# Second attention stage with rows of 3125 columns instead of 3200, and a last block of 53 rows

## The reference

```python
h = (x @ W).reshape(N, H, HD)
al_src = jnp.einsum('nhd,hd->nh', h, a_src)
al_dst = jnp.einsum('nhd,hd->nh', h, a_dst)
e = jax.nn.leaky_relu(al_src[src] + al_dst[dst], 0.2)
emax = jax.ops.segment_max(e, dst, num_segments=N)
ex = jnp.exp(e - emax[dst])
denom = jax.ops.segment_sum(ex, dst, num_segments=N)
out = jax.ops.segment_sum((ex / denom[dst])[:, :, None] * h[src], dst, num_segments=N)
...
y = _layernorm(out.reshape(N, DIM) + gat_b + res)
return _layernorm(jax.nn.gelu(y @ W1 + b1) @ W2 + b2 + y)
```

## Time and profile before

| | |
|---|---|
| median of 3 runs | 4212.96 us (4205.56 to 4214.2) |
| profiled execution | 4210.95 us, its span 4209.2 us |
| PE busy over the span | 3842.8 us, 91% |
| DVE | 2343.3 us, 56% |
| ACT | 2062.7 us, 49% |
| POOL | 589.5 us, 14% |
| L1027 and L1037 on DVE, 100 each | 355.1 us and 354.9 us |

### The profile page before, as it was taken

The page is one execution under the profiler, slowest core; times in us unless marked ns, Lnnn a source line. Parts: engine busy times, 40 slices in busy tenths (PEclk is TensorE's granted clock), DMA queues, the critical chain, the costliest instruction groups (busy, mean ns, idle before and its releaser), DMA issues. The chain is left out here.

```text
span 4209.2 us, 75724 instructions
## 1 busy us (share of the span) xinstructions
PE 3842.8 (91%) x27713; PEld 2926.6 (70%) x27714; DVE 2343.3 (56%) x4742; ACT 2062.7 (49%) x3697; POOL 589.5 (14%) x595
## 2 busy tenths in 40 slices
PE   4999969999999999599998888889979998996999
PEld 2555536666666666377777776678868887885888
DVE  7999835555555555399998898600002220002665
ACT  1555536666666666388887788500000010002554
POOL 0000001111111111100005566400000000000222
PEclk9999979999999999799999999999989998997999
DMA  2555562222222322433242332165644435554342
GB/s 66 213 228 220 212 205 96 103 84 106 103 84 96 108 88 71 167 111 107 98 169 89 102 104 88 62 182 145 146 146 150 147 128 179 145 145 152 141 145 99
DMA packets 185141, 550.29 MB, mean 131 GB/s; under 512 B 44903, under 2 KB 148529, under 8 KB 151217
## 3 DMA queue, kind: packets, MB, share of 16 engines
q1 hardware_dynamic: 184096, 540.23, 37.5%
q10 hardware_dynamic: 784, 6.55, 0.5%
HBM read 374.52 MB, written 172.19 MB: 130 GB/s over the span
## 5 line engine op out<-in xcount | busy, mean ns | idle before, releaser
L2005 PE MATMUL g_acc<-g_r,g_ct 128*128 128x256 f32 (+1 forms) x3750 | 862.9, 383 | 61.3 <-DMA g_r<-d_r 19.9
L931 ACT ACTIVATE a_sm<-a_p_t 128x1024 f32<-128x1024 f32 (+1 forms) x800 | 668.5, 836 | 370.6 <-PE a_p_t L874 370.4
L888 PE MATMUL a_p_o<-a_sm,a_v 128*64 128x128 f32 x10000 | 749.1, 281 | 85.6 <-ACT a_sumT L938 85.6
L888 PEld LDWEIGHTS a_p_o<-a_sm,a_v 128*64 128x64 f32 x10000 | 555.5, 137 | 377.1 <-issue 212.7
L2005 PEld LDWEIGHTS g_acc<-g_r,g_ct 128*128 128x128 f32 x3750 | 704.5, 192 | 161.2 <-issue 68.8
L874 PE MATMUL a_p_t<-ident,a_sm 128*128 128x128 f32 x5000 | 715.5, 281 | 41.3 <-ACT a_sm L925 26.1
L925 ACT ACTIVATE a_sm<-a_sm,a_negm 128x1024 f32<-128x1024 f32 (+1 forms) x600 | 706.8, 1178 | 85.0 <-DVE a_negm L991 84.6
L1011 DVE CUSTOM_DVE_ANT_0 a_sm<-a_p_s,a_full 128x400 f32<-128x400 f32 x800 | 429.3, 572 | 485.9 <-PE a_p_s L860 481.6
L874 PEld LDWEIGHTS a_p_t<-ident,a_sm 128*128 128x128 f32 x5000 | 559.1, 142 | 151.1 <-issue 128.0
L860 PE MATMUL a_p_s<-a_kt,a_q 64*128 64x400 f32 x1600 | 401.5, 560 | 34.2 <-DMA a_full<-d_logs 21.9
L1027 DVE SCALAR_TENSOR_TENSOR a_sm<-a_a_bc,a_al 128x3200 f32<-128x3200 f32 x100 | 355.1, 3551 | 34.0 <-DMA a_a_bc<-d_as 15.8
(11 more groups left out here) (244 smaller groups left out, 3926.7 us busy)
## 6 DMA issues: line engine op xcount, KB each, us to landing
a_mask<-d_full SPq DMA_DIRECT2D x75, 1600.0 KB, 6.8
g_ct<-d_ct SPq DMA_DIRECT2D x75, 1600.0 KB, 8.2
d_logs<-logs SPq DMA_DIRECT2D x25, 1664.0 KB, 6.9
a_full<-d_logs SPq DMA_DIRECT2D x25, 1664.0 KB, 7.5
d_ct<-ct SPq DMA_DIRECT2D x25, 1600.0 KB, 5.3
d_full<-a_full SPq DMA_DIRECT2D x25, 1600.0 KB, 5.4
a_a_bc<-d_as SPq DMA_DIRECT2D x10, 1600.0 KB, 9.6
a_q<-d_q SPq DMA_DIRECT2D x100, 64.0 KB, 2.2
```

The source lines that it names most:

```text
L888: m = nc.tensor.matmul(p_o[r:r + HD, 0:P], v[:, a, (p * heads + h) * HD:(p * heads + h + 1) * HD], sm[buf][:, a * P:(a + 1) * P], start=a ...
L931: nc.scalar.activation(sm[buf][:, a_row[u] * P:a_row[u + 1] * P], p_t[u % 2][:, 0:turns[u] * P], ACT.Copy).then_inc(s_copy, 1)
L2005: t = nc.tensor.matmul(acc[par][:, 0:width], ct[par][:, a * P:(a + 1) * P], r[:, a, :], start=a == 0, stop=a == NT - 1)
```

## The change

In the second attention stage (`dot` false) the row that is computed ends at column 3125 instead of 3200. Both DVE instructions get 3125 columns, the last part of the exponential 1077 instead of 1152. The last block of a row has 53 columns: it is turned as 128 rows by 53 columns into 53 rows of `p_t`, 53 rows are copied back, and 53 rows of `v` and of the turned block are multiplied. Loads, table sizes, buffers, semaphores and the first stage are as they were (in the first stage `width` is NPAD, so that every expression has its old value). The lines of the changed file are 3 or 4 higher.

```diff
+        width = NPAD if dot else N
+        exps = EXPS[:-1] + [width]
...
+        rows_in = lambda a: min(P, width - a * P)
...
-                        m = nc.tensor.transpose(p_t[u % 2][:, i * P:(i + 1) * P], sm[buf][:, a * P:(a + 1) * P], ident[:, :])
+                        m = nc.tensor.transpose(p_t[u % 2][0:rows_in(a), i * P:(i + 1) * P], sm[buf][:, a * P:a * P + rows_in(a)], ident[:, :])
...
-                        m = nc.tensor.matmul(p_o[r:r + HD, 0:P], v[:, a, (p * heads + h) * HD:(p * heads + h + 1) * HD], sm[buf][:, a * P:(a + 1) * P],
+                        m = nc.tensor.matmul(p_o[r:r + HD, 0:P], v[0:rows_in(a), a, (p * heads + h) * HD:(p * heads + h + 1) * HD], sm[buf][0:rows_in(a), a * P:(a + 1) * P],
...
-                    c = slice(EXPS[e], EXPS[e + 1])
+                    c = slice(exps[e], exps[e + 1])
...
-                    nc.scalar.activation(sm[buf][:, a_row[u] * P:a_row[u + 1] * P], p_t[u % 2][:, 0:turns[u] * P], ACT.Copy).then_inc(s_copy, 1)
+                    n_rows = rows_in(a_row[u + 1] - 1)
+                    nc.scalar.activation(sm[buf][0:n_rows, a_row[u] * P:a_row[u + 1] * P], p_t[u % 2][0:n_rows, 0:turns[u] * P], ACT.Copy).then_inc(s_copy, 1)
...
-                    v_.scalar_tensor_tensor(sm[buf][:, :], a_bc[:, h, 0, :], al[gp][:, g:g + 1], a_bc[:, h, 1, :], ALU.add, ALU.max).then_inc(s_lift, 1)
+                    v_.scalar_tensor_tensor(sm[buf][:, 0:N], a_bc[:, h, 0, 0:N], al[gp][:, g:g + 1], a_bc[:, h, 1, 0:N], ALU.add, ALU.max).then_inc(s_lift, 1)
...
-                    v_.tensor_tensor_reduce(out=sm[buf][:, :], in0=sm[buf][:, :], in1=mask[gp][:, :], scale=1.0, scalar=-3.0e38,
+                    v_.tensor_tensor_reduce(out=sm[buf][:, 0:N], in0=sm[buf][:, 0:N], in1=mask[gp][:, 0:N], scale=1.0, scalar=-3.0e38,
                                             op0=ALU.add, op1=ALU.max, accum_out=mx[:, buf % 2, 0:1]).then_inc(s_sfree, 1)
```

## The result

The changed kernel takes 4228.44 us (median of 8 runs, 4214.84 to 4232.3) where the kernel before takes 4208.48 (8 runs, 4203.68 to 4214.2). The ratio is 1.0043, 95% interval 1.0033 to 1.0052: slower, and outside the range that was given. The profiled execution has a span of 4228.3 us against 4209.2.

What follows compares the result with a forecast made beforehand. DVE was taken to bound the first stretch, DVE and the loop of PE and ACT in turn the second. Gains of 8.0 and 2 us from 4211 gave 4201, plus 2 for the median: 4203 us, range 4195 to 4219.

Steps and rivals of the forecast that it cites:

- DVE's 0.16 us a unit: DVE's two instructions, 3200 to 3125 columns: 0.16 us a unit less, 8.0 us over the first stretch's 50 units.
- The exponential: ACT's last exponential, 1152 to 1077 columns: 0.06 us a unit less, hidden in the first stretch, once a tile in the second.
- The copy and the last weighing of 53 rows: ACT's last copy and PE's last weighing, 53 rows for 128: nothing gained; for the weighing 0.17 us as upper bound.
- The last turn: PE's last turn, loading 53 columns of weights: 0.05 us a unit less, between nothing and 0.10, hidden in the first stretch.
- The full-clock tile of PE and ACT: Second stretch, loop of PE and ACT without a clock drop: down 0.11 us a tile, from 21.09 to 20.98 us.
- Second stretch, the sum: Where DVE's loop and that of PE and ACT run side by side: 2 us gained, between 2.4 and 7.0 less more drops.
- the kernel's present mix: Second stretch's 22 tiles by PE's clock: 9 at 20.98 us, 10 at 22.63, 3 at 23.81, taken to stay.
- The price of a very slow tile: Second stretch, tile with PE's clock at 0.50 after the restart: 23.81 us, 2.0 us more than a DVE-bound one.
- Rival D: Second stretch: PE locks into very slow tiles, 4235 us if all 22 are so, though the drift may turn; chance 0.11.
- the deciding share: Second stretch: share of very slow tiles from which the kernel is 0.2% slower, about 0.7.
- the 13 drops that I counted: Second stretch: 13 of 22 restarts of PE's weighing were followed by a drop of its clock, mostly every second one.
- Rival B: Second stretch: DVE carries its gain through, drops at every second tile or fewer; 15 us gained, 4198 us; chance 0.25.

Runs made afterwards that it cites:

- e4: The changed kernel with 14 small idle matmuls on PE in each tile's wait for the flip; 4190.27 us, ratio 0.9956 to the kernel before.
- e7: The kernel before with 14 small idle matmuls on PE in each tile's wait for the flip; 4205.64 us, ratio 0.9990.
- e8: The changed kernel with the Gelu on ACT and the down projection on PE two slots later; 4193.77 us, ratio 0.9963 to the kernel before.
- e11: The kernel before with the Gelu on ACT and the down projection on PE two slots later; 4207.49 us, ratio 0.9994.
- e3: The changed kernel with one more small copy a tile on ACT behind the Gelu; 4228.69 us, ratio 1.0050 to the kernel before.
- e5: The kernel before with the 53 rows alone, DVE and the exponential staying at 3200 columns; 4239.17 us, ratio 1.0053.
- e6: The changed kernel with 128 rows in the last turn, copy and weighing, only its time used; 4226.88 us, ratio 1.0013 to the kernel before.
- e1: The changed kernel with DVE's two instructions back at 3200 columns; 4241.93 us, ratio 1.0076 to the kernel before.

## Why the prediction was wrong

- *DVE's 0.16 us a unit:* right. 3475 and 3472 ns (3473 and 3468 forecast), 7.56 us a unit (7.55). The first stretch gave 6.7 of the 8.0 us; the lifts at the border of the passes wait for `a_bc` 1.1 us longer than they did.
- *The exponential:* right, 1188 ns (1187 forecast). *The copy and the last weighing of 53 rows:* nothing, right. *The last turn:* its weight load went from 0.14 to 0.12 us, so 0.02 us a unit, not 0.05, inside its bounds. The full-clock tile of PE and ACT became 21.00 us (20.98 forecast).
- *Second stretch, the sum:* this is the step that failed. The prediction kept "the kernel's present mix (9 fast, 10 slow, 3 very slow)" and took 2 us of gain. There were 17 very slow tiles, the mean tile went from 22.44 to 23.53 us, and the stretch lost 23.0 us. The price of a very slow tile (23.81 forecast, 23.90 measured) was right to 0.1 us; their number was not.
- *Rival D* named place, price and the deciding share (0.7; it was 17 of 21, 0.81), also that the drift might stop. I gave it 0.11. The tiles of the kernel before held the reason against that: 23.99, 23.94, 23.92 us is not a drift of constant size but one that halves, towards a length at which it stands still. Steps that shrink are the mark of a feedback; I took them for noise on a drift. Nor are the 13 drops that I counted of one kind: three began 0.70 to 0.85 us ahead of the restart and made the very slow tiles, one began just ahead of it, and the other nine fell behind it, with half clock for 3.4 us. The Trainium skill's account of a PE that idles between bursts and begins each burst at the low clock (TensorE: Matmul & The Clock Gate, HAM oscillation) pointed the same way, though the page tells it of longer waits than these 2.4 us. The changed kernel's trace agrees with it in 17 tiles of 21, and e4 shows that the wait is the cause.
- *Rival B* was the worth of the columns where the lock is out of the way, and right for that: 15.4 us in e4 against e7, 13.7 in e8 against e11. The kernel as changed did not come near it.
- What stays open: what exactly lets a locked row go. Half clock ahead of the restart was 0.85 us when the kernel before got free, while e3 was held at 1.05 us with a wait 0.12 us longer. What makes the first fall land inside the wait isn't known either: the same kernel, e5 or e6, locks in one run and not in the next. Nor was it tried how often each kernel enters the lock beyond the runs above.

## What to carry to other kernels

Where two loops of nearly equal length run side by side, price a gain on one by what the other does at each of its clock levels, and look at successive periods, not at their mean: lengths that converge tell of a lock. A wait of PE of some 2 us that comes back each period is worth breaking up first: here two idle matmuls did it, and so did moving the Gelu. Then the gain of the other engine arrived in full (15.4 and 13.7 us), and without it shorter instructions cost 20 us.

## What the runs showed of the hardware

- Five kernels whose full-clock tiles differ (21.00 us in the changed kernel, 21.17 in e3) or whose tiles with one drop do (22.61 us in e1, 22.68 in e5 and e6) settle on the same 23.89 us to 0.01 us. In the kernel before the falls came 23.89 us apart too, while its tiles took 23.99 and 23.94 us. So the length goes with the falls of the clock and not with the kernel's own work.
- Half clock stood for 6.9 us where it began inside a wait, 0.65 us ahead of the restart, and for 3.4 us where it began behind the restart.
- One small matmul behind the up projection lengthened the tile by 0.48 us, while the weight loads of 14 in a row took 3.03 us, 0.22 a matmul, and those of the 8 matmuls of a weighing turn take 0.85 us, 0.11 a matmul. The weighing goes to the two halves of `p_o` in turn and the 14 all to one half; that this is the reason is not shown.
- A transpose with 53 instead of 128 columns of weights is shown as `128*53`, a weighing with 53 rows as `53*64`; neither form cost more than the full one: in a unit of the first stretch the turn takes 0.32 us (0.33 before) and the two records of the weighing 0.43 us (0.43 before).
